# Layer 0's attention: probabilities and values split into two f32r parts, value products for two query tiles at once

## The reference, cut to what matters

```python
w = (qw - 8.0) * repeat(scales, 128, axis=0)       # for q, k, v and the output
q = h @ wq   # 32 heads of 128;  k, v = h @ wk, h @ wv   # 8 heads of 128
q, k = rope(q), rope(k)
scores = q @ k.T / sqrt(128), causal mask
ctx = softmax(scores) @ v                           # four q heads share one k, v head
x = x + gate * (ctx @ wo)
```

## Time and profile before

| | |
|---|---|
| median of 3 runs | 1751.47 us (1750.13 to 1751.73) |
| profiled execution | 1747.66 us, span 1745.8 us |
| granted clock of PE, mean | 0.978 |
| PE busy | 1654.7 us (95%) |
| PEld busy | 1337.1 us (77%) |
| DVE busy | 1170.5 us (67%) |
| ACT busy | 1044.1 us (60%) |
| POOL busy | 747.5 us (43%) |

### The profile page before, as it was taken

The page is one execution under the profiler, slowest core; times in us unless marked ns, Lnnn a source line. Parts: engine busy times, 40 slices in busy tenths (PEclk is TensorE's granted clock), DMA queues, the critical chain, the costliest instruction groups (busy, mean ns, idle before and its releaser), DMA issues. The chain is left out here.

```text
span 1745.8 us, 28527 instructions
## 1 busy us (share of the span) xinstructions
PE 1654.7 (95%) x10107; PEld 1337.1 (77%) x10123; DVE 1170.5 (67%) x2951; ACT 1044.1 (60%) x2261; POOL 747.5 (43%) x705
## 2 busy tenths in 40 slices
PE   4899999999999999999999799999988999999897
PEld 2699989999999989899988488878764555555476
DVE  5767677777777676777666743336777777776285
ACT  3477777877777777777777221114324666666553
POOL 3286585675856757567551300000352334321200
PEclk9999999999999999999999889999979999999998
DMA  6100000101010010000000512200230000000000
GB/s 195 38 14 24 26 25 20 31 13 38 13 31 25 19 37 13 25 19 25 13 19 7 166 46 70 68 1 19 84 83 13 1 1 1 1 1 1 1 19 31
DMA packets 75014, 55.82 MB, mean 32 GB/s; under 512 B 23502, under 2 KB 57998, under 8 KB 74874
## 3 DMA queue, kind: packets, MB, share of 16 engines
q1 hardware_dynamic: 73290, 53.21, 10.5%
q10 hardware_dynamic: 1584, 0.79, 0.2%
HBM read 51.88 MB, written 2.10 MB: 31 GB/s over the span
## 5 line engine op out<-in xcount | busy, mean ns | idle before, releaser
L778 PEld LDWEIGHTS psum<-a_probsT,a_v 128*128 128x128 f32 x2304 | 294.7, 191 | 25.6 <-issue 3.9
L778 PE MATMUL psum<-a_probsT,a_v 128*128 128x128 f32 x2304 | 299.2, 275 | 1.7 <-ACT a_probsT L988 1.6
L877 DVE CUSTOM_DVE_ANT_0 psum<-psum,a_keys_allowed 128x128 f32<-128x128 f32 (+7 forms) x256 | 195.7, 764 | 83.1 <-PE psum L78 74.5
L2109 ACT ACTIVATE a_probsT<-psum 128x512 f32<-128x512 f32 (+1 forms) x304 | 168.4, 588 | 106.1 <-PE psum L1976 67.4
L971 ACT ACTIVATE a_probs<-psum,a_neg_max 128x128 f32<-128x128 f32 (+7 forms) x256 | 190.7, 745 | 66.4 <-DVE a_neg_max L877 58.0
L980 ACT ACTIVATE a_probs<-a_probs,a_row_inv 128x128 f32<-128x128 f32 (+7 forms) x256 | 201.2, 786 | 27.8 <-DVE a_row_inv L884 27.6
L641 POOL TENSOR_TENSOR a_turned_pool<-a_q_sum,a_sine 64x512 f32<-64x512 f32 x62 | 79.3, 1279 | 286.8 <-DVE a_q_sum L863 285.6
L907 DVE TENSOR_TENSOR a_ctxT_lo<-psum,a_ctxT_hi 128x128 fp32r<-128x128 f32 x256 | 73.5, 287 | 172.7 <-ACT a_ctxT_hi L994 172.6
L988 ACT COPY a_probsT<-psum 128x512 f32<-128x512 f32 (+3 forms) x384 | 173.3, 488 | 18.8 <-PE psum L766 16.6
L897 DVE SCALAR_TENSOR_TENSOR a_sumT<-psum,a_scale_o,a_sumT 128x512 f32<-128x512 f32 x248 | 173.5, 741 | 0.9 <-PE psum L792 0.8
L766 PE MATMUL psum<-ident,a_probs 128*128 128x128 f32 x1152 | 168.9, 274 | 0.5 <-ACT a_vT L965 0.3
(11 more groups left out here) (394 smaller groups left out, 3891.3 us busy)
## 6 DMA issues: line engine op xcount, KB each, us to landing
a_raw_o<-in_L_attn_qw_o SPq DMA_DIRECT2D x32, 256.0 KB, 2.8
a_raw_q<-in_L_attn_qw_q SPq DMA_DIRECT2D x31, 256.0 KB, 3.6
mod1b_w<-in_L_wmod SPq DMA_DIRECT2D x4, 1024.0 KB, 6.2
mod0a_w<-in_L_wmod SPq DMA_DIRECT2D x3, 1024.0 KB, 12.8
mod0b_w<-in_L_wmod SPq DMA_DIRECT2D x3, 1024.0 KB, 7.5
f_raw<-in_L_ffn_down_w SPq DMA_DIRECT2D x10, 256.0 KB, 3.1
f_raw<-in_L_ffn_gate_w SPq DMA_DIRECT2D x10, 256.0 KB, 3.3
f_raw<-in_L_ffn_up_w SPq DMA_DIRECT2D x10, 256.0 KB, 3.6
```

Of the source, the lines that this page charges most:

```text
L778: last = nc.tensor.matmul(bank(use)[:, 0:P], v[:, g % 2, j, :], probsT[:, u % 2, j, :], start=(j == 0), stop=(j == i))
L877: nc.vector.tensor_tensor_reduce(out=scores, in0=scores, in1=keys_allowed[:, S - (i + 1) * P:S], scale=-1.0, scalar=-MASKED, op0=ALU.add, ...
L2109: nc.scalar.activation(probsT[:, s % SLOTS, hs[0]:hs[-1] + 1, first:HALF], scores_of(group, n, HALF - first), ACT.Exp).then_inc(exped.sem, 1)
```

## The change

Probabilities and v are each kept as a high and a low f32r part; the values are computed for two query tiles (a pair, 256 columns) at once, by three f32r passes for each key tile that both share, and one f32 matmul for the own keys of the odd tile (`own` is their turned probabilities in f32). ACT writes the high part of the turned probabilities, DVE then computes the low part (`low_probs`); a bank with turned probabilities is now taken out when DVE is done with it. The pair made of units u-3 and u-2 is computed in unit u, for odd u, so its last probabilities are turned in unit u-1 (`pair_due`). In all three engines the work on turned probabilities and values of a unit comes ahead of the partials and outputs; DVE takes the reciprocal of u+1 in unit u, after the low parts. Outputs move from odd to even units. v is single instead of double, with its split parts made by ACT (`high_v`) and DVE; both its turnings are in the group's first head (w = 1 and 4). k and v share one raw buffer; gate, rope and scale scratch lie in `sumT`. There is code for a case in which ACT takes some last partials (`extras`, `by_act_too`), and its list is empty, so it issues nothing.

```diff
     def outputs_due(h, p):
-        return [(h - 1, p - 1), (h - 1, p)] if h > 0 and p % 2 else []
+        return [(h - 1, p), (h - 1, p + 1)] if h > 0 and p % 2 == 0 else []
...
     def v_turn(h, p):
         g, w = h // REP0, h % REP0 * NT + p
-        if w == 25 and g < LAST_GROUP:
-            return g + 1, 0
-        if w == 1 and g > 0:
-            return g, 1
+        if w in (1, 4) and g > 0:
+            return g, 0 if w == 1 else 1
         return None
+
+    def pair_due(u):
+        if u % 2 == 0 or u < 3:
+            return []
+        h, i = units[u - 3]
+        return [(h, i // 2)]
...
         def load_kv(sp, name, g):
-            raw, arrived, made = (raw_k, k_in, wk_made) if name == "k" else (raw_v, v_in, wv_made)
-            if g:
-                sp.wait_ge(*made.of(g - 1))
+            arrived = k_in if name == "k" else v_in
+            raw = raw_v0 if (name, g) == ("v", 0) else raw_kv
+            if g == 1 and name == "k":
+                sp.wait_ge(*wk_made.of(0))
+            elif g:
+                sp.wait_ge(*(wv_made.of(g - 1) if name == "k" else wk_made.of(g)))
...
-                if h % REP0 == 0 and g + 2 <= LAST_GROUP:
+                if h % REP0 == 0 and g < LAST_GROUP:
+                    load_kv(sp, "v", g + 1)
+                if h % REP0 == 1 and g + 2 <= LAST_GROUP:
                     load_kv(sp, "k", g + 2)
...
-                if h % REP0 == 0 and g < LAST_GROUP:
-                    load_kv(sp, "v", g + 1)
...
                 if kind == "t":
-                    return turned_out.of(name)
+                    return lowered.of(name)
...
-            def values(u):
...
-                for j in range(i + 1):
-                    last = nc.tensor.matmul(bank(use)[:, 0:P], v[:, g % 2, j, :], probsT[:, u % 2, j, :],
-                                            start=(j == 0), stop=(j == i))
-                last.then_inc(filled.sem, 1)
+            def values(h, m):
+
+                g, use = h // REP0, ("pv", h, m)
                 wait_bank(use)
+                if h % REP0 == 0 and m % 2 == 0:
+                    pe.wait_ge(*v_taken.of((g, m // 2)))
+                pe.wait_ge(*lowered.of(pieces_of(h, 2 * m + 1)[-1]))
+                for j in range(2 * m + 1):
+                    split_products(nc.tensor, bank(use)[:, 0:2 * P], [part[:, j, :] for part in v_parts],
+                                   [part[:, j, :] for part in probsT], j == 0, False)
+                nc.tensor.matmul(bank(use)[:, P:2 * P], v[:, 2 * m + 1, :], own[:, :], start=False, stop=True
+                                 ).then_inc(filled.sem, 1)
```

PE's loop; its list of uses has the same order:

```diff
+                for due in pair_due(u):
+                    values(*due)
+                if u > 0:
+                    turn_probs(u - 1)
                 for due in q_partials(h, p) + kv_partials(h, p):
                     partial(*due)
                 for due in outputs_due(h, p):
                     output(*due)
                 if v_turn(h, p):
                     turn_v(*v_turn(h, p))
-                if u > 1:
-                    values(u - 2)
-                if u > 0:
-                    turn_probs(u - 1)
```

DVE:

```diff
+            def low_probs(u):
+                h, i = units[u]
+                for piece in pieces_of(h, i):
+                    first_key = piece[2] * TPH
+                    keys = slice(first_key, min(first_key + TPH, i + 1 - i % 2))
+                    turned = bank(("t", *piece))[:, 0:(keys.stop - keys.start) * P].rearrange("p (j q) -> p j q", q=P)
+                    dve.wait_ge(*turned_out.of(piece))
+                    nc.vector.tensor_tensor(probsT[1][:, keys, tile(i % 2)], turned, probsT[0][:, keys, tile(i % 2)].bitcast(F32),
+                                            ALU.subtract).then_inc(lowered.sem, 1)
...
             maximum(0)
+            invert(0)
             for u, (h, i) in enumerate(units):
                 p = u % NT
-                invert(u)
                 if u + 1 < len(units):
                     maximum(u + 1)
...
+                for due in pair_due(u):
+                    split_values(*due)
+                if u > 0:
+                    low_probs(u - 1)
+                if u + 1 < len(units):
+                    invert(u + 1)
                 for key, k in q_partials(h, p) + kv_partials(h, p):
-                    if k:
+                    if k and not by_act_too(key, k):
                         add_partial(key, k)
                 for due in outputs_due(h, p):
                     add_output(*due)
                 if v_turn(h, p):
                     take_v(*v_turn(h, p))
-                if u > 1:
-                    split_values(*units[u - 2])
```

ACT:

```diff
+                    if i % 2 and keys.stop == i + 1:
+                        keys = slice(first_key, i)
+                        nc.scalar.copy(own[:, :], bank(use)[:, tile(i - first_key)])
+                    turned = bank(use)[:, 0:(keys.stop - first_key) * P].rearrange("p (j q) -> p j q", q=P)
+                    nc.scalar.copy(probsT[0][:, keys, tile(i % 2)], turned).then_inc(turned_out.sem, 1)
...
+                for due in pair_due(u):
+                    high_values(*due)
+                if u > 0:
+                    take_turned(u - 1)
                 for key, k in q_partials(h, p) + kv_partials(h, p):
                     if k == 0:
                         take_first(key)
-                if u > 1:
-                    high_values(*units[u - 2])
-                if u > 0:
-                    take_turned(u - 1)
...
+                if v_turn(h, p):
+                    high_v(*v_turn(h, p))
```

More of the change, by code:

```diff
@@ L438, in layer0_attention_phase @@
         uses += first_uses(u)
+        uses += [("pv", *pair) for pair in pair_due(u)]
+        if u > 0:
+            uses += [("t", *piece) for piece in pieces_of(*units[u - 1])]
         for partial in q_partials(h, p) + kv_partials(h, p):
@@ L501, in layer0_attention_phase @@
         summed, ctx_lo, v_taken = count("summed", added_partials), count("ctx_lo", all_values), count("v_taken", v_turns)
+        lowered = count("lowered", pieces)
         ROPE_STEPS = ("sine", "cosine", "sum", "hi", "lo")
-        pool_roped = count("pool_roped", [(key, step) for key in pool_ropes for step in ROPE_STEPS])
+        pool_roped = count("pool_roped", [(key, step) for key in pool_ropes for step in ("extra",) * (key in extras) + ROPE_STEPS])
         dve_roped = count("dve_roped", [(key, step) for key in dve_ropes for step in ROPE_STEPS])
@@ L511, in layer0_attention_phase @@
         bank = lambda use: mem.bank[4 + use_at[use] % RING]
-        whole = lambda key: first_out.of(key) if key in FIRST_KEYS else summed.of((key, KT - 1))
+        whole = lambda key: first_out.of(key) if key in FIRST_KEYS else summed.of((key, KT - 2 if key in extras else KT - 1))
         roped = lambda key: (dve_roped if key in dve_ropes else pool_roped).of((key, "lo"))
@@ L540, in make_wkv @@
         def make_wkv(act, name, g):
-            raw, arrived, made, w = (raw_k, k_in, wk_made, wk) if name == "k" else (raw_v, v_in, wv_made, wv)
+            arrived, made, w = (k_in, wk_made, wk) if name == "k" else (v_in, wv_made, wv)
             act.wait_ge(arrived, 16 * (g + 2))
@@ L576, in first_weights @@
         def first_weights(act):
-            for n, (raw, arrived, made) in enumerate(((raw_q, q_in, wq_made), (raw_k, k_in, wk_made), (raw_v, v_in, wv_made))):
+            for n, (raw, arrived, made) in enumerate(((raw_q, q_in, wq_made), (raw_kv, k_in, wk_made), (raw_v0, v_in, wv_made))):
                 act.wait_ge(arrived, 32)
@@ L640, in rope @@
             engine.wait_ge(*whole(key))
+            if key in extras:
+                engine.wait_ge(*extra_out.of(key))
+                compute.tensor_tensor(x, x, extra[:, :], ALU.add).then_inc(counter.sem, 1)
+                engine.wait_ge(*counter.of((key, "extra")))
             compute.tensor_tensor(y[0:HH, :], x[HH:HD0, :], sine[HH:HD0, half(b)], ALU.mult)
@@ L701, in taken_out @@
                 if kind == "t":
-                    return turned_out.of(name)
+                    return lowered.of(name)
                 key, k = name
+                if key in extras and k == KT - 1:
+                    return extra_out.of(key)
                 return summed.of(name) if k else first_out.of(key)
@@ L838, in _ @@
                     turn_v(*v_turn(h, p))
-                if u > 1:
-                    values(u - 2)
-                if u > 0:
-                    turn_probs(u - 1)
-            values(len(units) - 2)
             turn_probs(len(units) - 1)
@@ L846, in _ @@
                 output(LAST_HEAD, n)
-            values(len(units) - 1)
+            values(*LAST_PAIR)
             for t in first_half:
@@ L936, in _ @@
                     take_v(*v_turn(h, p))
-                if u > 1:
-                    split_values(*units[u - 2])
-            split_values(*units[-2])
+            low_probs(len(units) - 1)
             for n in first_half:
```

(3 more changed lines are left out.)

92 lines of the change are left out of this document (53 added, 39 removed).

## The result

The change makes the kernel slower: 2129.94 us (median of 4 runs, 2118.57 to 2135.55) against 1751.60 beside it, a ratio of 1.215 with a 95% interval of 1.210 to 1.221. The direction is the one forecast. The time is 84 us above the number forecast and 20 us above the upper end of its range. The profiled execution took 2135.55 us, span 2133.7.

The account below looks back on a forecast made before the run. PE's stream bounds the kernel before, at 27.85 us a head; afterwards a ring through DVE, ACT and PE takes 37.3 in the mean, +292, with +3 for head 0, giving 2046 us, range 1950 to 2110.

Parts of the forecast that it names:

- The ring: Each unit's maximum, exponential, copy, subtraction, sums, next maximum run one after another without overlap: 37.6 us a head, mean 37.3.
- its terms: The forecast's step times laid out by unit, without v turns: 4.14 us in unit 0, 3.47 in unit 7, 36.8 together.
- DVE's new work: Twelve low-part subtractions a head out of PSUM, 5.2 us, raising DVE from 20.3 to 25.5 us a head.
- the prices taken: DVE's subtractions priced from the 128-wide one at 0.20 us and the 512-wide add at 0.62, 384 columns at 0.48.
- PE's relief: Value products on PE fall from 8.06 to 6.66 us a head: 1.4 saved, 45 us over 32 heads.
- In unit 7 the third pair, 2.0 us, starts early enough, since DVE has four sums to do meanwhile: PE's third value pair of a head was expected to add no wait to the ring in unit 7.
- The sum: Ring steps added for one head: 37.6 us, with 1.3 for PE, taken in unit 1.
- Its lateness would show only where DVE waits for outputs: With banks released by DVE, PE's lateness was expected to cost nothing, given over 10 us of slack a head.
- The clock rival: PE, busy 27 of 37 us in bursts, falls to the lower clock: 3.7 us a head more, +115, 2160; 10%.
- the two long pairs: PE's value pairs of 2.7 and 2.0 us a head, becoming near 5.0 and 3.7 at the lower clock.
- The signs of being wrong: DVE's idle time elsewhere than before the new subtraction, PE above 95%, or clock below 0.95 in the head loop.
- The edits priced at nothing: Scratch tiles in sumT and one raw buffer for k and v were expected to cost no time.

Follow-up runs that it names:

- e3_filler: The changed kernel plus six unread 512-column matmuls on PE before the outputs of every even unit with outputs: 2047.17 us, ratio 1.169.
- e5: e3_filler plus one unused 512-wide DVE addition in each of 256 units, right behind the maximum, where DVE waits for ACT: 2063.14 us, ratio 1.177.
- e6: e3_filler plus one unused 512-wide DVE addition in each of 256 units, behind the sums and ahead of the next maximum: 2211.76 us, ratio 1.262.
- e2: The kernel before, with values, turned probabilities and value split ahead of partials and outputs in all three engines, without the new split: 1910.46 us, ratio 1.092.
- e1: The changed kernel with all new work, but partials and outputs first, low parts last, as in the order before: 1913.56 us, ratio 1.093.

## Why the prediction was right in kind and short in size

- **The ring: right.** At full clock (e3_filler) the head takes 37.3 us, forecast 37.3, and the time is 2047, forecast 2046. That the two agree so closely is partly luck: by the table, with the v turns added, unit 0 is 0.3 us longer than its terms and unit 7 0.4, and the other six are shorter, unit 1 by 0.4. e5 and e6 show that it is a ring and not a full engine.
- **DVE's new work: right.** By shape, 150 to 1300 us (busy us, mean ns, idle before):

```profile
L940 DVE TENSOR_TENSOR a_probsT_lo<-psum,a_probsT_hi 128x512 fp32r<-128x512 f32 x112 | 77.5, 692 | 90.6 <-ACT a_probsT_hi L1029 88.9
...
L940 DVE TENSOR_TENSOR a_probsT_lo<-psum,a_probsT_hi 128x384 fp32r<-128x384 f32 x114 | 63.1, 553 | 46.3 <-ACT a_probsT_hi L1029 46.3
...
L940 DVE TENSOR_TENSOR a_probsT_lo<-psum,a_probsT_hi 128x128 fp32r<-128x128 f32 x114 | 32.4, 284 | 33.9 <-ACT a_probsT_hi L1029 33.9
```

  Less some 0.08 of overlap each these are 0.61, 0.47 and 0.20, the prices taken. DVE's 25.5 us a head by the forecast over 40.1 would be 64%; it is 444.78 / 700 = 64%.
- **PE's relief: right and worth nothing.** Passes of the pair go at 0.12 us at full clock.
- **"In unit 7 the third pair, 2.0 us, starts early enough, since DVE has four sums to do meanwhile": wrong, and the step that failed.** The sum has nothing for PE in unit 7, and nothing for the lower clock anywhere. DVE has its four sums in unit 6, but PE is held in that unit for a bank, so outputs, scores and pair all begin late (708.54), and the pair mostly runs at half pace. DVE waited 2.66 us in the mean and 3.65 in the rows shown; unit 7 is 2.0 us longer than its terms. At full clock it is 0.4 longer, so most of the wait is the clock and a smaller part the start. Another 0.66 us a head comes back in unit 4 with the clock, where the sum had nothing either for a maximum that waits for scores.
- **"Its lateness would show only where DVE waits for outputs": wrong.** PE's slack of 10 us a head was real as a sum, but it comes in pieces that end in a bank wait, 114 waits of L812 on L940 with 216.7 us in the loop. When DVE is done with a bank decides when PE's next piece starts.
- **The clock rival: right mechanism, too small a chance.** It had 10% and 2160; measured is the forecast plus 83 us, 2130. Its price was 3.7 us a head, 2.7 were measured (2129.94 - 2047.17 over 31). It put the cost in the two long pairs, though the 21 passes of unit 1 keep 0.12 to 0.16 in all heads and unit 4 has a part. Its own figures (5.0 + 3.7 in place of 2.7 + 2.0) add up to 4.0; it took 3.7 without saying why. What spoke against it was one stretch at 7.5 of 10 us with clock 1.00, and a busy share over 10 us says nothing of single gaps: here the lower clock came behind gaps of 2.3 us in unit 4 and of 2.4 to 2.9 in unit 6. The prediction had expected gaps "near 2.5 us" and had not said what such a gap does. Since the lower clock makes the ring longer and never shorter, the upper end of the range should have held it.
- **The signs of being wrong** that the prediction named have come in: clock under 0.95, and DVE's idle time mainly ahead of L930 (237.9 us), not of L940 (182.3). Only the first was a good sign. The wait of the ring itself stands at L930 in odd units, and in e3_filler, at the forecast time, the two are still equal (181.5 and 181.9).
- **Order and split.** Order alone costs 159 us (e2), split alone in the old order 162 (e1), both 378. At full clock (e3_filler) both cost 296, less than the sum of the two, 321: so that both together cost 57 more than the two apart comes with the clock, and without it the two overlap a little. The edits priced at nothing (shared raw buffer, scratch in `sumT`) leave no wait for a load among those listed for the loop.

Not tried: a bank ring with more than four places, which might loosen PE from DVE without fillers; the other four banks hold the scores, and the kernel would have to be laid out anew.

## What to carry to other kernels

Busy shares do not say whether an order will hold: follow one period through all engines, and put in each queue what somebody waits for ahead of what nobody waits for yet; moving ACT's exponential behind its copies (and one reciprocal of DVE) was worth 250 us here, 83 of them through the clock. When an engine that was the bound becomes one that waits, look for its longest single gaps and price what follows them at the lower clock too, if it lies in the new bound's path. If a gap can't be removed, work without use in it can pay: six matmuls in every second unit gave 83 us.

## What the hardware showed beyond this

A DVE addition with both inputs in SBUF is slow while POOL works. The added operation of e5 and e6, in all its 256 places (duration in ns: least, median, most):

```profile
L962 DVE TENSOR_TENSOR a_extra<-a_cosine x256: 680/1115/1749, 61.3 to 1269.1; 128x512 f32<-128x512 f32 x128
```
```profile
L984 DVE TENSOR_TENSOR a_extra<-a_cosine x256: 670/682/1474, 66.6 to 1420.3; 128x512 f32<-128x512 f32 x128
```

POOL in time, in e5:

```profile
704.01 1.29 POOL L670 TENSOR_TENSOR a_qT_lo<-a_q_sum,a_qT_hi 128x512 fp32r<-128x512 f32 x1
```

POOL's operation ends at 705.30; DVE's, begun at 704.19, ends at 705.85, 0.55 us later, as if it had begun only when POOL was done. The same addition at 708.91, with POOL idle, takes 0.69. DVE's operations with one full-size input in PSUM show no such spread: the q sums of e5 take 728 to 750 ns. The Trainium skill says that a DVE instruction with two SBUF inputs contends with a GpSimd instruction that reads SBUF, and calls the shared port pair an exclusive lock (SBUF — State Buffer, "Who interferes with whom"). These rows agree, and no run here varied it by itself.
